# Last feed-forward of a two-layer network: the down weights' low halves taken straight from memory, and shared chunks placed between the last routing steps

## The reference

```python
scores = jax.nn.sigmoid(x @ gate_w)
topk_w, topk_i = jax.lax.top_k(scores, TOP_K)          # 6 of 32 experts per token
g = jnp.einsum('td,edf->tef', x, wg)
u = jnp.einsum('td,edf->tef', x, wu)
act = jax.nn.silu(g) * u
routed = jnp.einsum('tef,efd,te->td', act, wd, combine)
shared = jax.nn.silu(hidden_states @ sg) * (hidden_states @ su) @ sd
return routed + shared
...
x = x + 0.5 * _L1_ffn_ref(_layernorm(x, axis=-1), ...)
x = x + _L1_attn_ref(_layernorm(x, axis=-1), ...)
x = x + 0.5 * _L1_ffn_ref(_layernorm(x, axis=-1), ...)
```

## Time and profile before

| | us |
|---|---|
| median of 3 timed runs | 1301.68 |
| lowest and highest | 1298.76, 1307.99 |
| span of the profiled execution | 1495.7 |

### The profile page before, as it was taken

One profiled execution on the slowest core, in us unless ns is written; L12 is line 12 of the kernel. 1 busy time (PEld: TensorE's weight loads), 2 busy tenths in 40 slices (PEclk: granted clock), 3 DMA queues, 4 the chain that ended last, 5 costly groups with the idle time before them and its releaser, 6 DMA issues.

```text
span 1495.7 us, 20198 instructions
## 1 busy us (share of the span) xinstructions
PE 1178.6 (79%) x6031; PEld 960.0 (64%) x6031; DVE 743.8 (50%) x2333; ACT 536.0 (36%) x1012; POOL 596.8 (40%) x579
## 2 busy tenths in 40 slices
PE   4799988979989898854768998897755436988884
PEld 4677755666778676633557987875434225978784
DVE  5553465564546536413445555678644214633443
ACT  2323344554533234321413433442303115644442
POOL 3661352211124213674550155662453730045554
PEclk9789999998989999865868999898875667998897
DMA  9523439400002573331426687760121212676676
GB/s 331 211 72 107 143 96 308 141 1 0 1 29 107 206 260 119 117 114 64 173 76 216 195 241 237 219 191 4 60 79 41 105 53 63 198 208 205 204 223 191
DMA packets 125302, 209.81 MB, mean 140 GB/s; under 512 B 15296, under 2 KB 104768, under 8 KB 123328
## 3 DMA queue, kind: packets, MB, share of 16 engines
q1 hardware_dynamic: 100624, 141.38, 28.7%
q0 software_dynamic: 24576, 67.14, 14.4%
HBM read 129.29 MB, written 101.19 MB: 154 GB/s over the span
## 4 chain that ended last, share of the span: by engine, by line
PE 48%; DVE 18%; issue 13%; another core or an unknown queue 10%; ACT 6%; POOL 3%; DMA 1%; SPq 0%; DVEq 0%; POOLq 0%; ACTq 0%
PE ps L910 15%; PE ps L932 6%; PE ps L877 5%; PE ps L817 4%; PE ps L829 4%; PE ps L889 3%; PE ps L1093 2%; PE ps L1100 2%; ACT xnt L1360 1%; PE ps L927 1%; PE ps L1244 1%; DVE HL L2047 1%; POOL xd L638 1%; PE ps L925 1%
## 5 line engine op out<-in xcount | busy, mean ns | idle before, releaser
L653 POOL DMA_INDIRECT G<-yd,slot_of x256 | 253.1, 989 | 424.6 <-issue 189.3
L638 POOL DMA_INDIRECT xd<-xnt,slot_of x256 | 251.4, 982 | 224.4 <-DVE slot_of L1986 136.9
L910 PE MATMUL ps<-WE,xT 128*128 x1016 | 200.7, 343 | 5.6 <-issue 3.9
L2102 DVE TENSOR_TENSOR hid<-hid,ps 128x192 f32<-128x192 f32 (+2 forms) x168 | 65.4, 389 | 247.9 <-ACT hid L1551 198.1
L910 PEld LDWEIGHTS ps<-WE,xT 128*128 128x128 f32 x1016 | 174.0, 202 | 9.9 <-issue 9.7
L1522 ACT ACTIVATE xT<-ps 128x512 f32<-128x512 f32 (+1 forms) x168 | 99.2, 590 | 156.9 <-PE ps L877 121.6
L877 PE MATMUL ps<-ident,xd_in 128*128 128x128 f32 x664 | 108.2, 287 | 44.2 <-ACT xT L1522 24.0
L2081 DVE SCALAR_TENSOR_TENSOR XT<-G,wt,XT 128x256 f32<-128x256 f32 x256 | 123.8, 494 | 27.5 <-DMA G<-yd,slot_of 17.0
L1551 ACT ACTIVATE hid<-ps 128x192 f32<-128x192 f32 (+2 forms) x168 | 60.4, 359 | 192.1 <-PE ps L910 139.9
L877 PEld LDWEIGHTS ps<-ident,xd_in 128*128 128x128 f32 x664 | 84.5, 148 | 60.6 <-issue 37.0
L1379 ACT ACTIVATE S<-ps 128x512 f32<-128x512 f32 (+1 forms) x72 | 42.6, 592 | 179.1 <-PE ps L817 140.1
(11 more groups left out here) (245 smaller groups left out, 2173.6 us busy)
## 6 DMA issues: line engine op xcount, KB each, us to landing
xd_in<-xd SPq DMA_DIRECT2D x164, 256.0 KB
yd<-yo SPq DMA_DIRECT2D x164, 256.0 KB
WE<-w SPq DMA_DIRECT2D x8, 1280.0 KB
W0E<-w0e SPq DMA_DIRECT2D x1, 4864.0 KB
xd<-xnt,slot_of POOLq DMA_INDIRECT x256
G<-yd,slot_of POOLq DMA_INDIRECT x256
W0E<-w0e SPq DMA_DIRECT2D x1, 3040.0 KB
XT<-x_in SPq DMA_DIRECT2D x4, 512.0 KB, 6.1
```

The costliest lines, as they stand in the source:

```text
L638: nc.gpsimd.indirect_dma_start(xd[f // 2][:, :], bass.IndirectOffsetOnAxis(ap=slot_of[:, t, k:k + 1], axis=0), xnt[:, t, :], None).then_in ...
L653: nc.gpsimd.indirect_dma_start(G[:, n % G_RING, :], None, yd[f // 2][0:min(ly.early[t][k] * 2, ly.TILES) * P, :], bass.IndirectOffsetOnAxi ...
L910: last = mm(dst, xT[:, q % 2, a, k, :], flat[:, bass.ds(expert[2 * q + a] + k * 2 * ly.H, 2 * ly.H)], start=(k == 0), stop=(k == KD - 1))
L2102: tt(hid[:, q % 2, 0:m, 0:ly.H], hid[:, q % 2, 0:m, 0:ly.H], src, ALU.mult).then_inc(TL.hid, 1)
```

## The change

Four things change, all of them in pass 3.

- `down_back` is gone. `down_low` now reads WDH and the weights both from SBUF, eight experts at a time, so four instructions of 2,048 columns instead of eight of 1,024. The groups are made in the order 1, 2, 3, 0, because WDH's first group shares its memory with XH of block 0.
- `gate_up` of a tile pair no longer waits for the low halves; only the first `down_rows` does.
- Chunks 1 and 2 stand between the routing steps of blocks 2 and 3: on PE `chunk(1)` after `next_rank(2)` and `chunk(2)` after `logits_of(3)`, where a chunk is its `gate_up` and the `down` of the chunk before. ACT and DVE follow. Chunks 0 to 3 all use PSUM banks 2 and 3.
- XH of blocks 1, 2 and 3, S3 and HL3 lie elsewhere; XH of blocks 2 and 3 now lie where QT and KB of the attention lay. SP's loads for pass 3 wait for the last `gate_up` instead of the last shared sum.

The core of the diff:

```diff
-            add(("s", f, b), ("s1", "s3")[f - 2], f, b, SH1, (2, 6))
+            add(("s", f, b), ("s1", "s3")[f - 2], f, b, SH1, (2, 6) if f == 2 or b >= 2 else (2, 2))
...
-            sp.wait_ge(CK.sum, GROUP["s", 3, 3] + 1)
+            sp.wait_ge(CK.gu, RUN["s", 3, 3][0][-1].i + 1)
             tiles(3)
...
-                    if f == 3 and i == 1:
-                        pe.wait_ge(ew_lo, PARTS0 + 8)
...
                         if q == q0:
-                            pe.wait_ge(ew_lo, PARTS0 + 8)
+                            pe.wait_ge(ew_lo, 4)
...
+                def chunk(k):
+                    gate_up(chunks[k], taken_over(chunks[k]))
+                    if k:
+                        down(chunks[k - 1])
+
...
-                gate_up(chunks[0], taken_over(chunks[0]))
+                chunk(0)
                 logits_of(2)
                 next_turn(3)
                 next_rank(2)
+                chunk(1)
                 logits_of(3)
+                chunk(2)
+                next_rank(3)
                 pe.wait_ge(F_NORM[3].lo, NB)
...
             def down_high(g):
                 if g == 0:
                     act.wait_ge(CK.gu, RUN["s", 3, 0][0][-1].i + 1)
-                    act.wait_ge(A1.add, 8)
                 fn(WDH[:, 8 * g:8 * g + 8, :], WDR[:, 8 * g:8 * g + 8, :], ACT.Copy).then_inc(ew_hi, 1)
-
-            def down_back(g):
-                act.wait_ge(ew_hi, g // 2 + 1)
...
+                for k in range(2, len(chunks)):
+                    silu(chunks[k])
+                    hidden(chunks[k])
+                    if k >= 4:
+                        down_high((1, 2, 3, 0)[k - 4])
...
-                rows = lambda v: v[:, 4 * g:4 * g + 4, :]
-                high = ps[:, A_BANK:A_BANK + 2, :].rearrange("p a (e n) -> p (a e) n", n=D)
-                tt(rows(WDL), rows(WDR), high, ALU.subtract).then_inc(ew_lo, 1)
+                rows = lambda v: v[:, 8 * g:8 * g + 8, :]
+                tt(rows(WDL), rows(WDR), rows(WDH).bitcast(F32), ALU.subtract).then_inc(ew_lo, 1)
...
                 chosen(f, 2)
+                prod(chunks[0])
+                low_hidden(chunks[0])
                 slots(f, 2, A_BANK)
                 split_low(3)
+                prod(chunks[1])
                 chosen(f, 3)
-                prod(chunks[0])
-                low_hidden(chunks[0])
+                low_hidden(chunks[1])
+                finish(chunks[1])
+                prod(chunks[2])
                 slots(f, 3, A_BANK)
```

More of the change, by code:

```diff
@@ L32 @@
 X2_RING = 3
-PARTS0 = 0
-HALVED0 = 0
 class Layer:
@@ L277, in program @@
         RN = inside("RN", [P, NT], F32)
-        xh31_at = upto[0]
-        XH[3, 1] = inside("XH3_1", [P, 2, KD, BT], F32R)
-        assert upto[0] <= tb_end, (upto[0], tb_end)
+        xh31_at = tb_end - 4 * 2 * KD * BT
+        assert upto[0] <= xh31_at, (upto[0], xh31_at)
+        XH[3, 1] = sb("XH3_1", [P, 2, KD, BT], F32R, xh31_at)
         X32 = G[:, 0:4, :].rearrange("p (k a) d -> p k (a d)", k=KD)
@@ L292, in program @@
         WDH = inside("WDH", [P, E1, D], F32R)
[L293 to L297, removed]
+        wdh_end = upto[0]
+        XH[3, 2] = sb("XH3_2", [P, 2, KD, BT], F32R, qt_at)
+        kb_at = qt_at + 4 * 2 * KD * BT
+        XH[3, 3] = sb("XH3_3", [P, 2, KD, BT], F32R, kb_at)
+        S3 = sb("S3", [P, 2, BT], F32, wdh_end)
+        assert wdh_end + 4 * 2 * BT <= qt_at
+        hl3_at = xt_at
+        HL3 = sb("HL3", [P, 2, 2, BT], F32R, hl3_at)
+        assert kb_at + 4 * 2 * KD * BT <= hl3_at and hl3_at + 4 * 4 * BT <= xh31_at
         WDF = sb("WDF", [P, E1, LY[1].EW], F32R, w_at)
@@ L363, in program @@
         hi_split, w_ready = sem("hi_split"), sem("w_ready")
-        ew_hi, ew_lo, ew_back = sem("ew_hi"), sem("ew_lo"), sem("ew_back")
+        ew_hi, ew_lo = sem("ew_hi"), sem("ew_lo")
         w0e_in, wsq_in, w1_in, sh1_in, att_in = sem("w0e_in"), sem("wsq_in"), sem("w1_in"), sem("sh1_in"), sem("att_in")
@@ L884, in hturned @@
                     if f == 3:
-                        pe.wait_ge(TL.hlo, HALVED0 + q - q0)
+                        pe.wait_ge(TL.hlo, q - q0)
                     for a in range(ly.tiles_in(q - q0)):
@@ L1316, in window @@
                 next_rank(2)
+                chunk(1)
                 logits_of(3)
+                chunk(2)
+                next_rank(3)
                 pe.wait_ge(F_NORM[3].lo, NB)
[L1319 to L1325, removed]
+                for k in range(3, len(chunks)):
+                    chunk(k)
+                    if k == 5:
                         expert_row(3, A_BANK)
@@ L1789, in window @@
                 split_high(2)
+                silu(chunks[0])
                 score(3, 2, A_BANK + 1)
                 rows(F_NORM[3], 3, XT[:, tiles_of(3), :])
+                hidden(chunks[0])
                 plain(3)
                 split_high(3)
+                silu(chunks[1])
                 score(3, 3, A_BANK + 1)
[L1795 to L1803, removed]
+                hidden(chunks[1])
+                for k in range(2, len(chunks)):
[3 more added lines that the diff above has]
+                        down_high((1, 2, 3, 0)[k - 4])
             act.wait_ge(consts_ready, 1)
@@ L2596, in window @@
                 chosen(f, 2)
+                prod(chunks[0])
+                low_hidden(chunks[0])
                 slots(f, 2, A_BANK)
                 split_low(3)
+                prod(chunks[1])
                 chosen(f, 3)
-                prod(chunks[0])
-                low_hidden(chunks[0])
+                low_hidden(chunks[1])
+                finish(chunks[1])
+                prod(chunks[2])
                 slots(f, 3, A_BANK)
-                for i in range(1, len(chunks)):
+                low_hidden(chunks[2])
+                for i in range(3, len(chunks)):
                     prod(chunks[i])
                     low_hidden(chunks[i])
-                    if i == 3:
+                    if i == 5:
                         experts(f, A_BANK)
@@ L2609, in window @@
                         finish(chunks[i])
-                    if i >= 3:
-                        down_low(i - 3)
-                for g in (5, 6, 7):
-                    down_low(g)
+                    if i >= 5:
+                        down_low(i - 5, (1, 2, 3, 0)[i - 5])
+                down_low(3, 0)
             nc.vector.memset(minus_half[:, :], -0.5)
```

14 lines of the change are left out of this document (4 added, 10 removed).

## The result

The changed kernel takes 1307.45 us in the median of 22 runs (1302.79 to 1310.30), the kernel before 1301.05 us beside it (22 runs, 1297.02 to 1307.99). The ratio is 1.0042 with a 95% interval of 1.0031 to 1.0053, by which the change costs 5.5 us; the two medians lie 6.4 us apart. That is less than 1%, but it is slower, and the median lies 0.45 us above the top of the predicted range.

A forecast was written before the change was run, and what follows sets the result against it. The prediction took POOL's scatters to bound the window, by 2.9 us. All terms were 0 except +0.4 us for block 2's later slots, giving 1302.1 us against the 1301.68 median, with a range of 1291 to 1307.

The forecast's parts named there:

- 2.9 to spare: End of the window: ACT free at 65.8, needed for the first pair at 68.7, so POOL's scatters bind by 2.9 us.
- I take 3.7 us: Scatter path: time for the last scatter to land, taken as 3.7 us from a pause in the stalled trace.
- the rival of the chunk path: Chunk path binds in the timed runs, so the change is faster: -2 to -12.5, middle -7, 1294.7 us; chance 0.28.
- about 5 us shorter: Chunks 1 and 2 moved ahead: chunk path becomes about 5 us shorter behind block 3's slots; worth 0.
- 0.4 late: Moved chunks ahead of block 2's slots: slots start 0.3 to 0.4 us late, taken as +0.4; bounds 0 to 2.2.
- the case that the prediction named for its high end: Block 2's slots: 2.2 us late if the logits come earlier in a timed run.
- All of this lies beside the scatters: it is worth 0 while they bind.: Copies to PSUM removed and four subtractions of 2.30 us, 9.2 us in all, on DVE: priced at 0.
- the mechanism as a rival: Subtractions with two SBUF inputs hold up POOL's scatters, slower: 1309 us and less; chance 0.05.
- Scaled to four of 2.30 that is 1 us: Subtractions beside scatters: 0.07 us seen for a DVE instruction of 0.69, scaled to four subtractions, gives 1 us.
- The row shows a tenth of that: Subtractions beside scatters: the trace row was said to show a tenth of the full blocking in the Trainium skill.
- If each held POOL for its whole length, the three that may fall in the scatters cost 6.9: 1309: Subtractions beside scatters: full holding by three of them would cost 6.9 us, giving 1309 us.
- the late slots: Block 3's slots come too late for POOL's scatters, slower: +10, 1312 us; chance 0.06.

The follow-up runs named there:

- e1_psum: Changed kernel with the subtraction alone undone: ScalarE copies four experts at a time to PSUM, VectorE subtracts from there, eight times; 1300.71 us, ratio 1.0008 to the kernel before.
- e2_late: Changed kernel with the four straight subtractions moved behind the last scatter's landing; 1300.60 us, ratio 1.0001 to the kernel before.
- e4_two: Changed kernel with each subtraction of eight experts made as two of four experts, back to back, inputs still in SBUF; 1306.62 us, ratio 1.0035 to the kernel before.
- e9_both: Changed kernel with low halves made through PSUM, plus 66 matmuls with unread results on PE behind the last chunk; 1301.01 us, ratio 0.9991 to the kernel before.
- e8_busy: Changed kernel with subtractions behind the last scatter's landing, plus 84 matmuls with unread results on PE behind the last chunk; 1300.06 us, ratio 0.9988 to the kernel before.

## Why the prediction was right and wrong

*What bounds the window: right in name.* POOL's scatters set its end, in all kernels. But the lengths laid out were off, since the profile at hand was stalled. I cut the unexplained waits out and kept the wait of 22.72 us for block 2's slots as real. It was not: block 2's slots are ready at 1041.2 in the second profile and POOL reaches them at 1045.3. "2.9 to spare" for ACT was really 8.4 (its idle time ahead of the first pair's copy there), and "I take 3.7 us" for the landing was 1.5 (below). POOL bound the window by far more than I said: PE stood idle for 15.50 us ahead of the first pair. That is why the rival of the chunk path fell with its 0.28.

ACT's timeline in the kernel before, second profile:

```profile
1102.31 1.03 ACT L1509 ACTIVATE ps<-WDH 128x1024 f32<-128x1024 f32 x1 [1.35 <-DVE WDF L2523]
1111.70 0.60 ACT L1522 ACTIVATE xT<-ps 128x512 f32<-128x512 f32 x1 [8.37 <-PE ps L877]
```

SP's timeline in the changed kernel, answering to the earlier trace rows; 1110.39 is 1.52 us after the last scatter's end (1107.91 + 0.96):

```profile
1110.39 4.56 SPq L547 DMA_DIRECT2D xd_in<-xd  x5
```

*The moved chunks: "about 5 us shorter" was right, and worth 0.* PE's last chunk ends 110.8 us after the first scatter before (1110.58 - 15.50 - 984.29) and 105.3 after (1113.47 - 27.52 - 980.65), 5.5 less. All of it became idle time of PE.

*Slots of block 2 "0.4 late": too small, and without effect.* They are ready 58.9 us after the first scatter instead of 56.9 (1039.55 - 980.65, and 1041.22 - 984.29). The delay is that of the sigmoid, which starts 48.1 after the first scatter instead of 46.1 (1028.70 - 980.65, and 1030.39 - 984.29): without the stalls the logits come earlier, the case that the prediction named for its high end. That end, 2.2, was the better value, but POOL asks for them at 1041.62, 2.1 us later still. DVE's wait for the ranks is gone, as said: base at 1034.15 follows at once. Block 3's slots, ready at 1054.71, are needed at 1072.8. The table load ahead of block 2's sigmoid, on ACT's timeline of the changed kernel, answering to the earlier trace rows:

```profile
1026.79 0.59 ACT L1384 ACTIVATE S<-ps 96x512 f32<-96x512 f32 x1
1027.40 1.28 ACT L1378 ACT_TABLE_LOAD   x1
1028.70 0.28 ACT L1378 ACTIVATE sc<-ps 128x128 f32<-128x128 f32 x1
```

Nothing but its 1.28 us stands between the silu and the sigmoid; this trace, too, doesn't agree with the further drain that the Trainium skill counts (ScalarE: Activation LUTs, "What ACT_TABLE_LOAD costs").

*The copies and the subtractions: the step that failed.* "All of this lies beside the scatters: it is worth 0 while they bind." The term was put at 0, and it was 6.0 us, the time by which four subtractions held the scatters. Lying beside the scatters is what cost it. I had the mechanism as a rival and gave it 0.05, on this reading: "Scaled to four of 2.30 that is 1 us", and of the rule that the later one blocks fully, "The row shows a tenth of that". The row shows no tenth. DVE's instruction at 1159.76 ends at 1160.45; the scatter at 1160.26 + 1.03 ends at 1161.29, 0.84 later. It had been held to the end there too. Of the 0.69 us only 0.19 was left when it started, and a scatter loses nothing for the first 0.13 of it (0.96 - 0.83), which leaves the 0.06 or 0.07 that I took for a price. The row was one sample in which the two hardly overlapped, and I scaled it by the instruction's length. The Trainium skill's rule (SBUF — State Buffer, section "Who interferes with whom": a DVE instruction with two SBUF inputs and a GpSimd one that reads SBUF contend, and the later one blocks fully) agrees with the long scatters laid beside DVE here. It isn't seen the other way round: the subtraction that started 0.45 us into the scatter at 1074.08 was not held. "If each held POOL for its whole length, the three that may fall in the scatters cost 6.9: 1309" was the right mechanism; all four fell among the scatters, at 0.9 to 2.1 us each.

*The range.* 1307.0 at its top left out most of the case that came. A full price of 6.9 us had been worked out, and the only reason not to reach to it was the misread row. That the median still came out within half a microsecond of the range is luck: the range reached that high for the late slots and the spread of the median, and neither brought the time there.

## What to carry to other kernels

Before an instruction that reads two inputs from SBUF is placed beside a run of GpSimd scatters that sets the pace, count it at its length less half of POOL's pace (2.28 - 0.63 us here, an estimate that fits instructions longer than that pace), not at nothing; one input from PSUM, or a place behind the scatters, takes the price away. A row that shows two engines beside each other prices a contention only by the time that both really overlap: compare ends, not lengths. And a profile that is 15% longer than the timed runs is to be taken again before slack is read from it.

## What the runs showed of the hardware that was not expected

- An indirect scatter that starts while a DVE instruction with two SBUF inputs runs ends 0.83 to 0.85 us after it, in every case laid side by side here; beside subtractions with one input from PSUM (1.21 us, e1_psum) none lasted over 0.97. A subtraction that starts while a scatter runs isn't held (2.28 us at 1074.53, as in e2_late beside no scatter). Why the one scatter of e4_two passed two pieces stays open.
- One execution of the kernel before took 1495.7 us in the profile, the second 1301.8, with the same instructions. What caused its stalls was not tried.
- After 4.50 us without work PE turned the first pair in 1.08 us, after 1.04 us in 0.63 (e9_both, e8_busy), although 66 and 84 matmuls had run just before. The granted clock was 0.50 and 1.00 then.
